# Row offsets of the experts read for several groups in one register load

## The reference, cut to what matters

```
sel = jax.nn.sigmoid(xt @ expert_sel.T)
sel_val, sel_idx = jax.lax.top_k(sel, TOP_K)
w = jnp.zeros((T, E)).at[jnp.arange(T)[:, None], sel_idx].add(sel_val)
h = jax.nn.relu(jnp.einsum('td,edh->teh', xt, keys))
out = jnp.einsum('teh,te,ehv->tv', h, w, values)
```

## Time and profile before

| what | value |
|---|---|
| time, median of 3 runs | 448.14 us (448.14 to 450.24) |
| span of the profiled execution | 477.4 us |
| PE busy in it | 388.7 us (81%) |
| DVE busy | 337.6 us (71%) |
| POOL busy | 294.4 us (62%) |
| ACT busy | 278.5 us (58%) |
| transfers | 54.36 MB, mean 114 GB/s |

### The profile page before, as it was taken

The page is one execution under the profiler, slowest core; times in us unless marked ns, Lnnn a source line. Parts: engine busy times, 40 slices in busy tenths (PEclk is TensorE's granted clock), DMA queues, the critical chain, the costliest instruction groups (busy, mean ns, idle before and its releaser), DMA issues.

```text
span 477.4 us, 10515 instructions
## 1 busy us (share of the span) xinstructions
PE 388.7 (81%) x2982; PEld 294.5 (62%) x2982; DVE 337.6 (71%) x1029; ACT 278.5 (58%) x821; POOL 294.4 (62%) x383
## 2 busy tenths in 40 slices
PE   8989999999999999999999886768684967795000
PEld 3756778777887768787877762446463756673000
DVE  2866788987989869899999767566574757787010
ACT  1343777766777767778788674455583956690000
POOL 6352547766777758778888877364645645655610
PEclk9999999999999999999999996898977989887555
DMA  8998121241231212311111112477553534311197
GB/s 228 337 211 203 44 56 47 57 139 52 76 88 48 67 40 64 98 59 62 64 57 52 61 69 79 138 243 214 186 180 123 167 116 140 115 56 35 30 266 187
DMA packets 33721, 54.36 MB, mean 114 GB/s; under 512 B 7836, under 2 KB 26734, under 8 KB 33165
## 3 DMA queue, kind: packets, MB, share of 16 engines
q1 hardware_dynamic: 23360, 29.25, 22.5%
q0 software_dynamic: 7872, 21.40, 14.0%
q10 hardware_dynamic: 2432, 3.04, 2.0%
HBM read 31.56 MB, written 25.73 MB: 120 GB/s over the span
## 4 chain that ended last, share of the span: by engine, by line
PE 50%; DVE 16%; issue 10%; another core or an unknown queue 6%; DMA 4%; ACT 4%; POOL 3%; SPq 1%; DVEq 1%; ACTq 1%; POOLq 0%
PE bank L1412 20%; PE bank L1369 7%; PE bank L1298 5%; PE bank L1395 3%; PE bank L1402 3%; DVE rows L1240 3%; PE bank L1550 2%; DVE vT L920 2%; DVE vT L1226 2%; DVE z_lo L932 2%; PE X L1519 2%; PE X L1531 2%; DMA xc_or_xin<-out 2%; PE bank L1280 1%
## 5 line engine op out<-in xcount | busy, mean ns | idle before, releaser
L1412 PE MATMUL bank<-vT,prob 128*128 128x256 f32 x512 | 116.1, 380 | 2.0 <-POOL prob L575 2.0
L649 POOL DMA_INDIRECT out<-vT,dest x80 | 78.5, 981 | 60.3 <-DVE vT L1226 37.9
L1412 PEld LDWEIGHTS bank<-vT,prob 128*128 128x128 f32 x512 | 94.9, 190 | 14.5 <-POOL prob L575 2.6
L552 POOL DMA_INDIRECT slot_rows<-rows,slot x64 | 65.0, 1015 | 17.1 <-issue 16.5
L575 POOL TENSOR_TENSOR prob<-prob,ginv 128x1024 f32<-128x1024 f32 x32 | 61.2, 1914 | 22.6 <-DVE ginv L1024 22.6
L546 POOL TENSOR_TENSOR rstd<-rstd,half_neg 128x1 f32<-128x1 f32 x64 | 35.7, 557 | 43.5 <-ACT rstd L699 41.8
L760 ACT ACTIVATE prob<-prob 128x1024 f32<-128x1024 f32 x32 | 33.8, 1057 | 20.9 <-DVE prob L992 14.3
L988 DVE TENSOR_REDUCE gmax<-X 128x32 f32<-128x1024 f32 x32 | 39.1, 1223 | 7.6 <-PE X L1332 6.9
L836 ACT ACTIVATE prob<-X 128x512 f32<-128x512 f32 x40 | 21.7, 589 | 36.5 <-remote 29.1
L1226 DVE SCALAR_TENSOR_TENSOR vT<-bank,wgt,vT 128x256 f32<-128x256 f32 x80 | 33.2, 477 | 11.9 <-remote 4.9
L1018 DVE TENSOR_REDUCE gsum<-prob 128x32 f32<-128x1024 f32 x32 | 38.7, 1210 | 3.6 <-ACT prob L760 3.5
(11 more groups left out here) (210 smaller groups left out, 870.5 us busy)
## 6 DMA issues: line engine op xcount, KB each, us to landing
xt<-x_tok SPq DMA_DIRECT2D x32, 128.0 KB, 2.1
values_s<-values SPq DMA_DIRECT2D x2, 2048.0 KB, 28.0
xc_or_xin<-slot_rows SPq DMA_DIRECT2D x26, 130.0 KB
out<-out POOLq DMA_DIRECT2D x4, 832.0 KB, 14.7
xc_or_xin<-x_cm SPq DMA_DIRECT2D x3, 1024.0 KB, 9.2
t<-slot_rows SPq DMA_DIRECT2D x16, 130.0 KB
keys_s<-keys SPq DMA_DIRECT2D x1, 2048.0 KB, 13.6
t<-slot_rows SPq DMA_DIRECT2D x24, 65.0 KB
```

The costliest lines, as they stand in the source:

```text
L552: g.indirect_dma_start(out=slots_d, out_offset=bass.IndirectOffsetOnAxis(ap=slot[:, t % RB, r:r + 1], axis=0), in_=rows[:, t % RB, r, :], ...
L649: g.indirect_dma_start(out=out, out_offset=bass.IndirectOffsetOnAxis(ap=dest[:, n % (2 * NB), k:k + 1], axis=0), in_=yb[:, n % NB, k, :], ...
L1412: mm = m.matmul(av_p, pr[:, j, :], vT[:, b % 2, j, :], start=(j == 0), stop=(j == KB - 1))
```

## The change

SyncE makes 8 register loads where it made 20. One load brings the offsets of groups 0 and 1, one those of groups 2 to 5, one those of 6 and 7, one those of 8 to 11, and four those of the pairs of groups of half tiles. The transfers, their order and the waits ahead of them stay, but the offsets of groups 0 and 1 are all loaded ahead of the wait for `scattered`. A load for whole tiles takes every second word of the schedule (8 or 16 words; before it was 2 in group 0 and 4 in the others), one for two groups of half tiles takes 14 adjacent words (before it was 6).

```diff
-            starts = [sp.alloc_register(f"start{k}") for k in range(2 * GROUP)]
-
-            def load_group(n):
-                if n == 0:
-                    start = loaded(sp, starts[:FIRST_BY_SP], entries(1, n)[:, 0:2 * FIRST_BY_SP:2], NE * CAP)
-                    for i in range(RB):
-                        sp.wait_ge(scattered[i], 2 * 16 * len(range(i, NT, RB)))
-                elif parts(n) == 1:
-                    start = loaded(sp, starts[:GROUP], entries(1, n)[:, ::2], NE * CAP)
-                else:
-                    start = loaded(sp, starts[:2 * (GROUP - 1)], entries(1, n)[:, 0:2 * (GROUP - 1)], NE * CAP)
+            starts = [sp.alloc_register(f"start{k}") for k in range(4 * GROUP)]
+
+            def whole_starts(n, groups):
+
+                at = n * 2 * GROUP
+                part = 2 + at // P
+                words = sched_i[part:part + 1, at % P:at % P + 2 * GROUP * groups:2]
+                return loaded(sp, starts[:GROUP * groups], words, NE * CAP)
+
+            def half_starts(n):
+
+                at = n * 2 * GROUP
+                part = 2 + at // P
+                words = sched_i[part:part + 1, at % P:at % P + 2 * (2 * GROUP) - 2]
+                both = loaded(sp, starts[:4 * GROUP - 2], words, NE * CAP)
+                return both[0:2 * GROUP - 2] + both[2 * GROUP:]
...
+            def load_whole(n, start):
+                buffer_free(n)
+                for k in range(tiles_by_sp(n)):
+                    sp.dma_start(row_buffer(n)[:, k, :], slots_d[bass.ds(start[k], P), :]).then_inc(ld_rows[n % XB], 16)
...
-            for n in range(GROUPS):
-                if n == NO_PAD_GROUPS:
+            start = whole_starts(0, 2)
+            for i in range(RB):
+                sp.wait_ge(scattered[i], 2 * 16 * len(range(i, NT, RB)))
+            load_whole(0, start[0:GROUP])
+            load_whole(1, start[GROUP:])
+            for first, groups in ((2, 4), (6, 2), (NO_PAD_GROUPS, 4)):
+                if first == NO_PAD_GROUPS:
                     sp.wait_ge(pads_done, 16 * (PB + PR))
-                load_group(n)
+                start = whole_starts(first, groups)
+                for g_ in range(groups):
+                    load_whole(first + g_, start[g_ * GROUP:(g_ + 1) * GROUP])
+            for first in range(WHOLE_GROUPS, GROUPS, 2):
+                start = half_starts(first)
+                for g_ in range(2):
+                    load_halves(first + g_, start[g_ * (2 * GROUP - 2):(g_ + 1) * (2 * GROUP - 2)])
```

More of the change, by code:

```diff
@@ L448, in _, with buffer_free @@
             sp.wait_ge(sched_out, 1)
-            starts = [sp.alloc_register(f"start{k}") for k in range(2 * GROUP)]
-            def load_group(n):
-                if n == 0:
-                    start = loaded(sp, starts[:FIRST_BY_SP], entries(1, n)[:, 0:2 * FIRST_BY_SP:2], NE * CAP)
-                    for i in range(RB):
-                        sp.wait_ge(scattered[i], 2 * 16 * len(range(i, NT, RB)))
-                elif parts(n) == 1:
-                    start = loaded(sp, starts[:GROUP], entries(1, n)[:, ::2], NE * CAP)
-                else:
-                    start = loaded(sp, starts[:2 * (GROUP - 1)], entries(1, n)[:, 0:2 * (GROUP - 1)], NE * CAP)
+            starts = [sp.alloc_register(f"start{k}") for k in range(4 * GROUP)]
[10 more added lines that the diff above has]
+                return both[0:2 * GROUP - 2] + both[2 * GROUP:]
+            def buffer_free(n):
                 if n == NB:
@@ L465, in load_group, with tiles_by_sp, load_halves @@
                     sp.wait_ge(rebuilt, n - XB + 1)
[L466 to L472, removed]
-            for n in range(GROUPS):
-                if n == NO_PAD_GROUPS:
-                    sp.wait_ge(pads_done, 16 * (PB + PR))
-                load_group(n)
+            def tiles_by_sp(n):
+                return FIRST_BY_SP if n == 0 else GROUP - 1 if n >= BY_ACT else GROUP
+            def load_whole(n, start):
+                buffer_free(n)
+                for k in range(tiles_by_sp(n)):
+                    sp.dma_start(row_buffer(n)[:, k, :], slots_d[bass.ds(start[k], P), :]).then_inc(ld_rows[n % XB], 16)
+            def load_halves(n, start):
+                buffer_free(n)
+                for k in range(tiles_by_sp(n)):
+                    for r in range(2):
+                        sp.dma_start(row_buffer(n)[r * HALF:(r + 1) * HALF, k, :],
+                                     slots_d[bass.ds(start[2 * k + r], HALF), :]).then_inc(ld_rows[n % XB], 16)
+            start = whole_starts(0, 2)
[5 more added lines that the diff above has]
+                if first == NO_PAD_GROUPS:
+                    sp.wait_ge(pads_done, 16 * (PB + PR))
+                start = whole_starts(first, groups)
[5 more added lines that the diff above has]
+                    load_halves(first + g_, start[g_ * (2 * GROUP - 2):(g_ + 1) * (2 * GROUP - 2)])
             for i in range(NB):
```

## The result

The changed kernel takes 453.22 us (median of 4 runs, 452.38 to 453.68) against 448.22 us before (448.14 to 450.24): ratio 1.0103, 95% interval 1.0082 to 1.0125. It is slower by 1.0% (the bare medians are 1.1% apart), above the forecast range (445.7 to 450.5).

A forecast was written before the change was run, and what follows sets the result against it. The prediction took GpSimd's sends to bound the expert part, their end set by when the first starts. It added +0.47 us on the first send and 0 elsewhere to 448.14, making 448.6 us, with a range of 445.7 to 450.5.

The forecast's parts named there:

- What bounds the kernel: Expert part: GpSimd sends with next to no gap once it has its first tile; SyncE's crawl belongs to the profiled execution.
- The first load, +0.47 us: SyncE ahead of group 0: 8 words in place of 2 delay the first transfer and first send by 0.47 us.
- The upper end, +1.38: Largest delay allowed for group 0's first transfer, +1.38 us, with the 8-word load at 1.73 us.
- 0.5 earlier: Group 1 loses its own load, so its transfers come 0.5 us earlier and the last two fills up to that.
- Groups 2 to 5, 0.0 us: One 16-word load, taken as 1.04 us, replaces one of 4; with group 1's shift, group 2's transfers move by 0.0 us.
- The upper end of 3.6: Largest delay allowed for group 2's transfers, +3.6 us, with spaced words priced at 0.217 us each.
- The slower rival: Spaced words cost by the word in the 16-word load ahead of group 2, delaying GpSimd's second group: 450.4 us; chance 0.10.
- the 1.3 us forecast: Slack of about 1.3 us by which group 2's rows could come late before delaying the outputs of group 1.
- TensorE's order: TensorE's fixed order puts group 2's transposes ahead of the outputs of group 1, so late group 2 rows hold these back.
- Groups 6 to 19, nothing: Later merged loads are hidden behind eight buffers and cost or bring nothing; uncovered, a saved load is worth at most 0.87 us.
- The faster rival: Rows still pace the first groups; groups 3 to 5 come 1.0 to 3.1 us sooner, giving 446.1 us; chance 0.18.

The follow-up runs named there:

- e1: Kernel before with twenty unused register loads added on SyncE, which don't appear in the trace, so it serves as a second profile of before; ratio 0.9993.
- e9: Changed kernel with GpSimd's last two fills moved behind the sends of group 0; ratio 1.0004 to the kernel before.
- e10: Kernel before, one register load per group, with GpSimd's last two fills moved behind the sends of group 0; ratio 0.9998.
- e11: Kernel before with one of the last two fills in its old place and the other behind the sends of group 0; ratio 0.9989.
- e2: Kernel before with only the first merge: one load of 8 words for groups 0 and 1, then one load per group; ratio 1.0008.
- e8: Kernel before with one load of 8 words for groups 2 and 3 and one for 4 and 5, otherwise one per group; ratio 1.0010.
- e3: Kernel before with only the second merge: one load of 16 words for groups 2 to 5, otherwise one per group; ratio 1.0092, 452.85 us.
- e12: Kernel before with the last two fills right behind the two small ones, not waiting for group 1's rows; ratio 1.0014.
- e5: Changed kernel with 14 unused TensorE matmuls between the keys of group 1 and the transposes of group 2; ratio 1.0076 to the kernel before.
- e6: Changed kernel with the outputs of group 1 ahead of the transposes of group 2 on TensorE; ratio 1.0065 to the kernel before.
- e4: Kernel before up to group 5, one load each, with the merges of the change from group 6 on; ratio 1.0000.

## Why the prediction was wrong

*What bounds the kernel.* Right. The stretches in which SyncE crawled belonged to that one profiled execution: e1, the same program, has a span of 446.0 us. GpSimd's own pace does set the end: in e1 the sends take 105.9 us from the first start to the last, where 101.9 would be without any gap. e9 and e10 close the gaps of over half a microsecond between sends, e11 all but one, but the two fills, 2.6 us, now stand there, and no gain is left that can be measured.

*The first load, +0.47 us.* The term was mis-sized. The step "The nearest row is SyncE's own spaced load of 4, so I take 0.87 + 4 x 0.014 = 0.92 us" took its slope from ScalarE's adjacent words, while the words to be read were spaced. Measured: 1.86 us, the first transfer 1.36 us later (2.45 us behind the start of the load against 1.09). The upper end, +1.38, was right. In time it hardly counts: the first send moves by 0.6 us in e2, and e2 as a whole by 0.0008, with at most 0.0034 in its interval. Group 1's rows landed 0.3 us later than in e1, not 0.5 earlier (the first fill, which they release, starts 8.84 us behind the first load against 8.52 in e1). The 200 ns a register of the Trainium skill (page "Runtime: NRT & Kernel Launch", section "Instruction fetch mechanics"), which that page gives for loads from device memory and by which the prediction estimated 1.6 and 3.2 us, comes near the measured 1.86 and 3.37 us for spaced words in on-chip memory; it does not fit the 14 adjacent words, at 0.10 us a word. The trace of before reached only four spaced words.

*Groups 2 to 5, 0.0 us.* This is the step that failed. "By the same sums it takes 0.87 + 12 x 0.014 = 1.04 us" is 3.37 us in the trace. Its place in the program is the same in three kernels, and there 4 spaced words took 1.07 us (e1), 8 took 1.87 (e8) and 16 took 3.41 (e3). Group 2's last transfer starts at 12.3 us behind the first load in place of 8.6 in e1: 3.7 us late. The upper end of 3.6 meets that by luck: the two loads alone make 2.7 (11.3 us in e9, where no issue hangs), and 1.0 is the hung issue. The slower rival, given 0.10, was thus the right case. But its price, 450.4 us, was still 2.8 us short, and its reason left two things out.

First, the fills. The prediction saw that GpSimd's fills start when group 1's rows land, and let them cost nothing. In e1 group 2's transfers are issued by the time the first fill begins, and e12 shows them hang and land late when fills go ahead of them. The 3.4 us load puts them behind the first fill. One of them then takes 1.40 us to issue, and from issue to use it is 5.4 us in place of 2.6 in e9. e9 takes the meeting away and leaves the load: the loss goes, as far as can be measured. So it is the late issue and the fills together. The load alone costs nothing that can be measured; the slack in front of it, which e1 shows as 2.5 us at the outputs of group 1, is larger than the 1.3 us forecast. e8 spends that slack to the last 0.1 us and still costs nothing that can be measured.

Second, the clock. TensorE idles 4.2 us for group 2's rows, and the granted clock is 0.50 behind that. The transposes, outputs and keys then take 0.93, 0.95 and 0.47 us longer (1.97, 2.08 and 2.46 against 1.04, 1.13 and 1.99 in e1). e5 takes this back in the trace; in time it brings 1.2 us, which its interval doesn't separate from nothing.

The pieces add up in the trace. The transposes of group 2 start 5.4 us later than in e1 (17.7 against 12.3 behind the first load); less 2.5 of slack, plus 0.93 and 0.95 at the low clock, that is 4.8 us. GpSimd's second group of sends starts 4.7 us later (23.2 against 18.5), and the time is longer by 4.6 us by the ratio, 5.0 by the medians.

*TensorE's order.* Right as a mechanism: the outputs of group 1 stood behind group 2's transposes. In e6's trace the second group's sends come 3.6 us earlier, and group 2's own lateness shows a group later; the 1.7 us in time are not separated from nothing.

*Groups 6 to 19, nothing.* Right (e4, 1.0000), though the load of 16 ahead of group 8 took 3.98 us: eight buffers cover it. The faster rival has nothing for it: in e9 the last transfer of group 5 is issued at 17.5 us behind the first load in place of 21.4 in e1, and nothing was gained.

What stays open: how much of the 2.8 us between issue and use is waiting behind the fills' traffic and how much behind the first sends, which run beside them in the changed kernel; e9 moves the fills, but lets rows and sends still meet. And the price of a load of spaced words was seen only in the loads that the kernels use, not on an idle SyncE.

## What to carry to other kernels

These register loads of spaced words weren't made cheaper by reading more at once: from 4 words on they were paid by the word, so a merged load only moved later words ahead of the first transfer that waits for it. Price a merged step from rows of its own kind, spaced words separately from adjacent ones, and then ask which burst of other traffic the work behind it will now fall into: here the transfers had been issued just ahead of two fills, and 2.7 us of delay cost 4.6 because they lost that place. The merges behind several buffers of slack cost and brought nothing.

## What the runs showed of the hardware that was not expected

SyncE's register loads of 2, 4, 8 and 16 spaced words took 0.66, 0.87, 1.86 and 3.37 us ahead of the fills; beside other transfers some took much longer (4 words 2.53 us in e1, 8 words 3.33 in e9). Three loads of 14 adjacent words took 1.34 to 1.41 us, less than 8 spaced ones, and a fourth 1.82. Transfers issued behind GpSimd's two fills took up to 1.40 us to issue in place of 0.33, and 5.3 to 5.7 us from the last issue to use, in place of 2.6 (e8, e12 and the changed kernel against e9). One profiled execution of the kernel before had a span 31 us longer than another of the same program (477.4 and 446.0 us), with register moves of up to 0.7 us in it, while the times of the two kernels agree (0.9993).
